# Setup loads, modulation products, gates and relu squared in an adaLN transformer block: what moves when they change place

## What is computed

```python
mod = silu(c) @ wmod                   # c (2, 512), wmod (512, 6*512): sa, ca, ga, sb, cb, gb
ga, gb = sign * max(abs, 0.25)         # of each gate
h = layernorm(x) * (1 + ca) + sa
q, k, v = silu(h @ wq), sigmoid(h @ wk), h @ wv      # 4 heads of 128
f = 1 - k;  theta = pi * cumsum(sign(f - 0.5))       # rotation by 0 or pi: a sign
S = S * f + k v^T;  o = q S            # gated scan over 4096 steps
o = layernorm(o * sigmoid(h @ wg1 @ wg2)) * norm_w
x = x + ga * (o @ wo)
h = layernorm(x) * (1 + cb) + sb
hp = h shifted by one step in time
r = sigmoid((mu_r * h + (1 - mu_r) * hp) @ W_r.T)
k = (mu_k * h + (1 - mu_k) * hp) @ W_k.T
x = x + gb * r * (square(relu(k)) @ W_v.T)
```

## Time and profile before

| | us |
|---|---|
| median of 3 runs | 1885.78 |
| lowest and highest | 1882.69, 1887.09 |
| the profiled execution, its own time | 1883.84 |
| its span in the profile | 1881.9 |
| TensorE busy in the span | 1836.1 |
| VectorE, ScalarE, GpSimd busy | 1457.9, 696.8, 391.4 |
| granted TensorE clock, mean | 0.994 |

### The profile page before, as it was taken

One profiled execution on the slowest core, in us unless ns is written; L12 is line 12 of the kernel. 1 busy time (PEld: TensorE's weight loads), 2 busy tenths in 40 slices (PEclk: granted clock), 3 DMA queues, 4 the chain that ended last, 5 costly groups with the idle time before them and its releaser, 6 DMA issues. The chain is left out here.

```text
span 1881.9 us, 56458 instructions
## 1 busy us (share of the span) xinstructions
PE 1836.1 (98%) x24873; PEld 1648.7 (88%) x24873; DVE 1457.9 (77%) x2885; ACT 696.8 (37%) x1360; POOL 391.4 (21%) x309
## 2 busy tenths in 40 slices
PE   5899999999999999999999999998999999999999
PEld 5789998999989998899988999887888888888887
DVE  4577777677777777777777777778899889889886
ACT  2243334333343333333333333343334434433433
POOL 1001100111011100111001110012244444344343
PEclk9899999999999999999999999999999999999999
DMA  7010100001000010001100011002111111111110
GB/s 280 3 47 25 47 25 25 24 28 43 25 25 24 33 39 25 24 25 36 35 25 24 25 37 35 24 26 68 60 53 68 68 51 62 68 57 57 68 57 34
DMA packets 42650, 84.88 MB, mean 45 GB/s; under 512 B 2324, under 2 KB 2856, under 8 KB 42408
## 3 DMA queue, kind: packets, MB, share of 16 engines
q1 hardware_dynamic: 38552, 74.46, 11.3%
q10 hardware_dynamic: 3856, 6.82, 1.0%
HBM read 47.72 MB, written 33.55 MB: 43 GB/s over the span
## 5 line engine op out<-in xcount | busy, mean ns | idle before, releaser
L130 POOL TENSOR_TENSOR ln_rs<-ln_ve,mhalf 128x2 f32<-128x2 f32 x64 | 71.2, 1113 | 1011.1 <-DVE ln_ve L125 1011.1
L324 POOL TENSOR_TENSOR xs<-xs,y 128x512 f32<-128x512 f32 x64 | 83.5, 1305 | 368.3 <-DVE y L697 368.3
L1099 PE MATMUL bank<-hT_hi,wq_hi 128*128 128x256 f32 x512 | 152.5, 298 | 4.4 <-DVE wq_lo L1043 4.4
L1099 PE MATMUL bank<-hT_hi,wk_hi 128*128 128x256 f32 x512 | 151.4, 296 | 0.0
L730 DVE TENSOR_TENSOR Tot<-Tot 128x256 f32<-128x256 f32 (+2 forms) x192 | 47.1, 245 | 129.4 <-PE lvl L1176 99.1
L136 DVE TENSOR_SCALAR xn<-xs,ln_mv,ln_rs 128x512 f32<-128x512 f32 x128 | 123.5, 1006 | 29.5 <-POOL ln_rs L130 29.5
L1099 PE MATMUL bank<-hT_lo,wq_hi 128*128 128x256 f32 x512 | 146.3, 286 | 0.0
L1099 PE MATMUL bank<-hT_hi,wq_lo 128*128 128x256 f32 x512 | 145.9, 285 | 0.0
L1099 PE MATMUL bank<-xk_hi,fk_hi 128*128 128x256 f32 x512 | 145.1, 283 | 0.6 <-DVE xk_lo L829 0.6
L1099 PE MATMUL bank<-xk_hi,fk_lo 128*128 128x256 f32 x512 | 144.9, 283 | 0.0
L1099 PE MATMUL bank<-xk_lo,fk_hi 128*128 128x256 f32 x512 | 144.9, 283 | 0.0
(11 more groups left out here) (179 smaller groups left out, 5630.2 us busy)
## 6 DMA issues: line engine op xcount, KB each, us to landing
xs<-in_L_attn_x SPq DMA_DIRECT2D x32, 512.0 KB, 3.6
x_scratch<-xs SPq DMA_DIRECT2D x32, 512.0 KB, 3.2
xs<-x_scratch SPq DMA_DIRECT2D x32, 512.0 KB, 3.5
out<-xs SPq DMA_DIRECT2D x31, 512.0 KB, 2.8
mod_raw<-in_L_wmod SPq DMA_DIRECT2D x4, 1024.0 KB, 15.6
mod_raw<-in_L_wmod ACTq DMA_DIRECT2D x2, 1024.0 KB, 14.2
raw_q<-in_L_attn_wq ACTq DMA_DIRECT2D x1, 1024.0 KB, 12.5
raw_k<-in_L_attn_wk SPq DMA_DIRECT2D x1, 1024.0 KB, 14.3
```

Of the source, the lines that this page charges most:

```text
L130: pool.tensor_tensor(out=ln["rs"][:, :], in0=ln["ve"][:, :], in1=mhalf[:, :], op=ALU.pow).then_inc(ln["rstd"], 1)
L324: pool.tensor_tensor(out=dst, in0=dst, in1=y[:, ch, :], op=ALU.add).then_inc(x2_sb, 1)
L1099: last = pe.matmul(dst, lhs(a, s), rhs(b, s), start=(t == 0), stop=(t == len(terms) - 1))
```

## The change

- **Loads.** SA, wq, wg1, wg2, wo and GB leave ScalarE's queue; SyncE issues all the large ones in the order CA, SA, wq, wk, (wait for the first modulation product) wv, wg1, wg2, x of block 1, wo, GA, GB, CB, SB. ScalarE runs one sigmoid on a constant column (`warm`) ahead of the one that is needed. W_k and W_r are issued at the end of block 2.
- **Prologue.** xn of block 1 is turned and the mean of wo made ahead of the gate rows; ScalarE makes h of block 1 ahead of the gate sigmoids.
- **Modulation products.** GA stays behind the near scores; GB, CB and SB stand after the second q rows, the first k rows and the second k rows of block 0, each ahead of a level product. `second_mods` and gate a's diagonal move behind VectorE's update of level 16, centring wo becomes `centre_wo` in the old place, all of wo's low part is made after g1's.
- **Gates.** Gate a is spread in block 0 in the two places where gate b was. Gate b's diagonal is made at the end of block 0 and spread in blocks 1 and 2, one batch each, after the k rows.
- **relu squared.** The square is a ScalarE activation right behind each relu; VectorE has none.

Context lines are thinned out, and the code is shifted left by eight columns:

```diff
@@ -182,12 +182,13 @@
 csig = at("csig", [P, B * KT], 134.5)
-csil = at("csil", [P, B, KT], 134.625)
+csil = at("csil", [P, B, KT], 1.46875)
 mean_m = at("mean_m", [P, P], 135)
...
 nwm = at("nwm", [P, KT, P], 148)
-diag = [at(f"diag{n}", [P, B * KT, P], kb) for n, kb in enumerate((154, 186))]
+diag = [at(f"diag{n}", [P, B * KT, P], kb) for n, kb in enumerate((178, 202))]
+warm = at("warm", [P, 1], 206.5)
 graw, gmag, gsgn = (at(name, [P, 2 * B * KT], 206 + n / 8) for n, name in enumerate(("graw", "gmag", "gsgn")))
@@ -286,11 +287,17 @@
         mod_load(CA)
+        mod_load(SA)
+        rows_in(w_raw["q"], env["wq"], w_in["q"])
         rows_in(w_raw["k"], env["wk"], w_in["k"])
...
         rows_in(w_raw["v"], env["wv"], w_in["v"])
+        rows_in(w_raw["g1"], env["wg1"], w_in["g1"])
+        rows_in(w_raw["g2"], env["wg2"], w_in["g2"])
         ln_load(sp, ln, xf, 1)
+        rows_in(w_raw["o"], env["wo"], w_in["o"])
         mod_load(GA)
+        mod_load(GB)
         mod_load(CB)
@@ -494,6 +501,11 @@
 
+        def square(m, pair):
+            part = rl[:, 2 * pair:2 * pair + 2, :].rearrange("p k t -> p (k t)")
+            act.wait_ge(relu, 2 * m + pair + 1)
+            act.activation(part, part, ACT.Square).then_inc(sq, 1)
+
         def ka_high(m, pair):
@@ -519,20 +531,19 @@
                 q_gate(n + 1, 1 - par, pair)
-            if n == 0:
-                gate_copy(0, bank[0])
-                gate_copy(1, bank[1])
             k_and_f(n + 1, 1 - par, 0)
+            if n == LAST - 1:
+                weight_high("k")
+            k_and_f(n + 1, 1 - par, 1)
+            if n in (1, 2):
+                gate_copy(n + 1, bank[1])
+            v_copy(n + 1, 1 - par, 0)
+            spread_diagonal(n)
+            merge_32(n, par)
             if n == 0:
...
                 act.copy(W["o"][0][:, :, :], w_raw["o"][:, :, :]).then_inc(w_hi["o"], 1)
-            if n == LAST - 1:
-                weight_high("k")
-            k_and_f(n + 1, 1 - par, 1)
-            v_copy(n + 1, 1 - par, 0)
-            spread_diagonal(n)
-            merge_32(n, par)
             if n == LAST - 1:
@@ -540,7 +551,7 @@
             if n == 0:
-                gate_copy(2, bank[3])
+                gate_copy(0, bank[3])
             for ch in range(chunks_kept(n)):
@@ -548,8 +559,8 @@
             if n == 0:
-                gate_copy(3, bank[1])
-                act.wait_ge(w_lo["o"], KT)
+                gate_copy(1, bank[1])
+            if n == 2:
                 for name in "kr":
@@ -562,8 +573,10 @@
             relu_of(0, 0)
+            square(0, 0)
             spread_diagonal(n)
             relu_of(0, 1)
+            square(0, 1)
             merge_32(n, par)
@@ -577,7 +590,9 @@
             relu_of(1, 0)
+            square(1, 0)
             relu_of(1, 1)
+            square(1, 1)
             ogt_high(n, 1)
@@ -586,6 +601,7 @@
                     relu_of(m, pair)
+                    square(m, pair)
                 for pair in range(2):
@@ -607,10 +623,8 @@
         act.dma_start(vrows[(B + 2) * KT:(B + 3) * KT, :], env["mu_k"].rearrange("(k p) -> k p", p=P)).then_inc(small_in, 16)
-        act.dma_start(mod_raw[SA][:, :, :], wmod[:, SA * E:(SA + 1) * E].rearrange("(k p) n -> p k n", p=P)).then_inc(mod_in[SA], 16)
-        for name in ("q", "g1", "g2", "o"):
-            act.dma_start(w_raw[name][:, :, :], env["w" + name].rearrange("(k p) n -> p k n", p=P)).then_inc(w_in[name], 16)
-        act.dma_start(mod_raw[GB][:, :, :], wmod[:, GB * E:(GB + 1) * E].rearrange("(k p) n -> p k n", p=P)).then_inc(mod_in[GB], 16)
+        act.wait_ge(step_pool, 2)
+        act.activation(warm[:, :], mhalf[:, 0:1], ACT.Sigmoid)
         act.wait_ge(vec_sb, 1)
@@ -629,11 +643,11 @@
         g1_high(0)
+        h_affine(1)
         for ch in range(NC):
...
         act.copy(mean_sb[:, :], lbank[0][:, :]).then_inc(mean_copied, 1)
-        h_affine(1)
         for n in range(LAST):
@@ -691,7 +705,7 @@
             dve.wait_ge(rstdo, n + 1)
-            if n == 0 or fresh(n):
+            if n == 0:
                 dve.wait_ge(gab_set, 2)
@@ -836,11 +850,6 @@
 
-        def square(m, pair):
-            part = rl[:, 2 * pair:2 * pair + 2, :]
-            dve.wait_ge(relu, 2 * m + pair + 1)
-            dve.tensor_tensor(out=part, in0=part, in1=part, op=ALU.mult).then_inc(sq, 1)
-
         def ka_low(m, pair):
@@ -878,6 +887,8 @@
                                      op0=ALU.add, op1=ALU.mult).then_inc(gates_set, 1)
+
+        def centre_wo():
             dve.wait_ge(mean_copied, 1)
@@ -907,10 +918,10 @@
                 if m == 1 and n == 0:
+                    centre_wo()
+                if m == 16 and n == 0:
                     second_mods()
                     spread_ready(0)
-                if m == 4 and n == 0:
-                    spread_ready(1)
                 if 1 < m <= 16:
@@ -926,14 +937,13 @@
                     weight_low("k", [m // 32])
-                if n == 0 and m == 32:
-                    split_low_o([0])
             apply_next(n + 2)
...
             if n == 0:
-                split_low_o([1, 2, 3])
+                split_low_o(range(KT))
+                spread_ready(1)
             if n > 0:
@@ -982,8 +992,6 @@
             ln_var(dve, ln, n + 2)
-            square(0, 0)
-            square(0, 1)
             weight_low("v", [1, 2, 3])
@@ -1004,8 +1012,6 @@
             apply_next(n + 3)
-            square(1, 0)
-            square(1, 1)
             ogt_low(n, 1)
@@ -1015,8 +1021,6 @@
             if m > 1:
-                for pair in range(2):
-                    square(m, pair)
                 for pair in range(2):
@@ -1230,10 +1234,9 @@
                 pe.wait_ge(gate_sb, 2)
-                for i in range(2, 6):
-                    mod_product(i, bank[1])
+                mod_product(2, bank[1])
             if n == 1:
-                pe.wait_ge(gab_set, 4)
+                pe.wait_ge(gab_set, 2)
             if n > 0:
@@ -1247,25 +1250,32 @@
             rows_of("q", 1, 2, "q")
+            if n == 0:
+                mod_product(3, bank[1])
             level_product(n, par, 3)
-            if n == 0:
-                pe.wait_ge(h_full, 8)
-                spread_gates(0, 0, bank[0])
-                spread_gates(0, 1, bank[1])
             if n > 0:
...
             rows_of("k", 0, 4, "k")
+            if n == 0:
+                mod_product(4, bank[1])
             level_product(n, par, 4)
...
             rows_of("k", 1, 4, "k")
+            if n == 0:
+                mod_product(5, bank[1])
+            if n in (1, 2):
+                pe.wait_ge(ogt_lo, 2 * n)
+                spread_gates(1, n - 1, bank[1])
             level_product(n, par, 5)
...
             wait(pe, ogt_lo, 2 * n)
-            if n == 0:
-                pe.wait_ge(gab_set, 2)
             v_rows(0)
             level_product(n, par, 6)
+            if n == 0:
+                pe.wait_ge(diag_set, 1)
+            if n in (1, 2):
+                pe.wait_ge(gab_set, n + 2)
             v_rows(1)
@@ -1277,7 +1287,7 @@
                 pe.wait_ge(q_sb, 2 * (n + 2))
-                spread_gates(1, 0, bank[3])
+                spread_gates(0, 0, bank[3])
             pe.wait_ge(level, NU * (n + 1))
@@ -1296,7 +1306,7 @@
             else:
-                pe.wait_ge(gab_set, 3)
+                pe.wait_ge(gab_set, 1)
             for ch in range(chunks_kept(n)):
@@ -1307,7 +1317,7 @@
                 pe.wait_ge(gate_sb, 2 * (n + 2))
-                spread_gates(1, 1, bank[1])
+                spread_gates(0, 1, bank[1])
             pe.wait_ge(s_mid, n + 1)
@@ -1429,20 +1439,21 @@
         g1_rows()
-        pe.wait_ge(g1_lo, 1)
-        pe.wait_ge(w_lo["g2"], 1)
-        pe.wait_ge(v_sb, 2)
-        for ch in range(NC):
-            gate_rows(ch)
+        pe.wait_ge(k_f, 2)
+        pe.wait_ge(v_sb, 1)
+        t1(1)
         pe.wait_ge(mod_set, 2)
...
         last.then_inc(mean_ready, 1)
-        pe.wait_ge(k_f, 2)
-        pe.wait_ge(gate_sb, 1)
-        t1(1)
+        pe.wait_ge(g1_lo, 1)
+        pe.wait_ge(w_lo["g2"], 1)
+        pe.wait_ge(v_sb, 2)
+        pe.wait_ge(h_full, 8)
+        for ch in range(NC):
+            gate_rows(ch)
         for n in range(LAST):
```

## The result

| | before | after |
|---|---|---|
| median in the comparison | 1885.30 us (4 runs) | 1873.28 us (4 runs, 1871.95 to 1875.95) |
| ratio to before | 1 | 0.9939, 95% interval 0.9922 to 0.9956 |
| the profiled execution | 1883.84 us | 1875.95 us |
| its span | 1881.9 us | 1874.0 us |

The change gained 12.0 us at the medians; forecast were 1870.9 us and a gain of 14.9. So a ledger made from them adds up to 7.9, and most of the edits were also run one by one.

What follows compares the result with a forecast made beforehand. TensorE, busy in 98% of the span, was taken as the bound. Terms -6.0 - 0.9 - 4.1 + 0 + 1.2 + 0 + 0.1 - 5.2 = -14.9 us took the median from 1885.8 to 1870.9 us, range 1865 to 1879.

Steps and rivals of the forecast that it cites:

- Part 1: Start: loads on one queue and warm-up activation start the first product near 7.3 us, the stop keeping its length; -6.0 us.
- B: Rival at the start: the stop shortens, second product ends near 12.3 us, 3 us better, 1867.9 us; chance 0.15.
- C: Rival at the start: the stop lasts while the DMA engines are full, only 1 us gained, 1875.9 us; chance 0.12.
- Part 2: Prologue: transposes and the mean of wo ahead of the gate rows cover the wait for g1's low part; -0.9 us.
- Part 3: Block 0: spreading the four modulation products lets instruction packets arrive in time, 9.7 us for 13.8; -4.1 us.
- Rival A: Products stay instruction-bound wherever they stand (0 for -4.1) and the clock falls once more (+2.1): 1877.1 us; chance 0.20.
- one slow stretch: Block 0's clock: one stretch at half clock as before, 0 us, between -1.7 and +4.2.
- Part 4: Blocks 0 to 2: moved gate spreads net 0; VectorE late for diagonal, level of 64 and g1's low part, +1.2 us.
- Part 5: Squares on ScalarE: crossing stalls shrink to 1.9 and 1.7 us (-2.4), no clock falls (-2.8); together -5.2 us.
- rival D: Crossing: the clock falls all the same and only the 2.4 us come, 1873.7 us; chance 0.08.
- the signs that I had named for being right: They included, for the crossing, both stalls below 2 us with the clock at 1.0.
- E: Rival in the feed-forward blocks: Square needs another activation table, +39 us in all, 1910 us; chance 0.03.

Runs made afterwards that it cites:

- experiment 8: Only the prologue's new order (transposes and mean ahead of the gate rows), on the kernel before: 1886.35 us, ratio 0.9991.
- Experiment 3: The changed kernel with the four later modulation products in a row again behind the near scores: 1877.30 us, ratio 0.9946.
- experiment 4: The changed kernel with modulation products 128 columns per matmul, a quarter of the instructions: 1887.98 us, ratio 1.0005.
- experiment 6: The changed kernel with modulation products 64 columns per matmul, half the instructions: 1871.18 us, ratio 0.9908.
- experiment 5: The changed kernel with the W_k and W_r loads issued earlier in block 2, ahead of its v copies: 1874.14 us, ratio 0.9921.
- kernels 7 and 8: 7: only the squares on ScalarE, on the kernel before: 1884.98 us, ratio 0.9985. 8 is experiment 8.
- experiments 1, 2, 8 and 4: 2: the changed kernel with the squares back on VectorE: 1878.92 us, ratio 0.9953. The others are experiment 1, experiment 8 and experiment 4.
- experiment 1: The kernel before with only the loads on one queue and the warm-up sigmoid: 1881.87 us, ratio 0.9970.

## Why the prediction was right, and where it was not

**Part 1, the start (-6.0 forecast, -5.3 in the ledger, -5.2 by itself).** Right in its mechanism: the next wait was for data, then the stop that keeps its length (7.67 us after the product's start, 7.43 before; 7.12 to 7.76 in all nine profiles that have it). That refutes B, in which it shortens, and C, in which it lasts until the DMA engines are free. By its own numbers, 7.3 for 13.58, the term was -6.3 and not -6.0. The term's fault: the first product started at 8.05, not 7.3. The sum of the rates was right (1.62 MB had moved at 7.2 us here too), but 1.95 MB had moved when the product started: I took the bytes moved for the landing of this matrix, while part of them belonged to the loads issued behind it, by my reading.

**Part 2 (-0.9, measured -1.3; -1.55 by itself).** Right in direction, and larger than the one wait it was read from; the interval of experiment 8 just reaches no change. The same stretch differs by up to 0.8 us between profiles of kernels with the same code there, which is as much as the excess. The g_lo entry of 0.9 that the view of waits still has belongs to the gate rows of the next block, in block 0.

**Part 3 (-4.1).** Right, and the strongest step. Its stated 9.7 us holds 4.5 us of idleness, where two pieces of 2.1 are 4.2; the trace has 4.3, and the products with it take 9.5 us, for 14.0 before: the first product kept its stop (2.09), the second lost it, the third handed it to the level product behind it (2.21), the fourth lost it. Experiment 3 puts the four back in a row and gets 7.6 us of idleness and 3.8 us more in block 0. Experiments 4 and 6 remove instructions, leave every byte of data where it is, and the stops of these products vanish. That speaks against the rule of the Trainium skill, "Runtime: NRT & Kernel Launch", Instruction fetch mechanics, that the crossing of a 16 KiB block is "mostly hidden": here each costs 1.6 to 2.7 us when what lies between two crossings runs for 1.25 us. Rival A falls with it. The clock fell in two places in block 0, 53 to 59 (0.72) and 70.8 to 75.4 us (0.63), where one slow stretch had been taken, each behind a stop of 2 us: this is the +2.1 for one more slow stretch, inside my bounds, and the reason why block 0 gave 3.8 of 4.9.

**Part 4 (gates 0, VectorE +1.2).** The gates' two spreads came back as 0.97 and 0.96 us in blocks 1 and 2: net 0. VectorE was late by 0.42 us for the diagonal and 0.22 for the level of 64, and the wait for g1's low part grew from 0.7 to 0.9: together 0.9 of the +1.2, each near what was said (0.5, 0.4, 0.3). What failed here is a sentence of this part: W_k and W_r "move to block 2, a thousand microseconds before use". I priced the loads by their use, not by what else was on the DMA queues. They drain into block 3 and delay the instructions of a level product: 0.64 us of idleness, block 3 +0.9 (experiment 5).

**Part 5, the crossing (-5.2 forecast; -2.8 measured by itself, -2.1 in the ledger).** This is the step that failed. Half of it was right: the Kt stall went from 3.1 to 0.8 (forecast 1.9), and the clock stayed at 1.00 behind it. The other half was wrong. I let the ogT stall shrink to 1.7 because two squares leave the place ahead of its low part, and beside that counted the 1.4 us that the clock gives back behind the Kt stall. But TensorE meets the ogT stall behind that stretch. What it gained there it waits for again: its way from the end of the Kt stall to the ogT stall went from 20.29 to 18.89 us, VectorE's from 23.20 to 21.26, and the stall only from 2.9 to 2.4. The stretch from TensorE's arrival at Kt to the end of the ogT stall still gave 4.2 us, for the 3.8 that these terms come to. What is missing is the clock. Behind the ogT stall it fell (0.72, as before), where I had expected it to stay up. And it fell once more, at 1277, in this profile and not in the one before. So half of rival D came true, and of the signs that I had named for being right, this is the one that did not show. Checked against the ledger: -5.2, +1.4 for the slow stretch that stayed, +0.7 for the ogT stall, -1.1 for the Kt stall, +2.3 for the one at 1277 (the wo products took 5.33 us for 3.00), -0.6 for a wait for xk's low part that is then covered, makes -2.5, and -2.1 is what stands there. The feed-forward half cost nothing but 0.3 us at its end, and E did not happen: Square (0.63 us for 128 x 512) runs on the table that was loaded.

**What stays open.** The fall behind the 2.2 us stall at the start of the crossing, at 1277 in the changed kernel, shows in ten of the twelve profiles, kernels 7 and 8 among them, which have the loads and the products as before; the first wo rows there take 4.5 to 5.4 us. Only the kernel before and experiment 4 kept the clock (3.00 and 2.98 us), and both profiles are of executions faster than their kernel's median. The ogT stall shows the same: the clock fell behind it in eight profiles (stalls of 2.4 to 2.9 us) and stayed up in four, experiments 1, 2, 8 and 4 (2.25 to 2.42 us). So nothing shows the fall at 1277 to be a cost of the change, my reading of the earlier trace rows, that a stall of 2.2 us is safe, was drawn from an exception, and what decides it I can't say: the code of the stretch at 1277 is the same in all twelve. The steady blocks take 39.17 us in all profiles but those of the kernel before and of experiment 1, which have 39.11: kernels 7 and 8 don't touch these blocks either, so the +1.4 us of the ledger can't be put down to one edit. Where it comes from stays open.

**The sum.** The forecast median, 1870.9, is 2.4 us from the measured 1873.28, with the missing 3 us of the crossing and 0.9 of block 3 against it. In its favour worked that issue idleness of the row of products was 7.2 us in the one profile I read, and 7.6 to 9.2 in four other kernels that have it in a row: with the products spread it is 4.3 to 5.1 in four profiles, so spreading saves about 3.4 us in the mean, for the 2.9 of the two profiles compared. The single edits come to 5.2, 2.8 and 1.7 us by themselves, and the products to 1.3 (ratios) or 3.8 (block 0): 11.0 to 13.5, beside 12 to 14 for the whole. That the total came out so near is in part luck: the crossing fell short by half, and the two profiled executions, which the parts are read from, differ by only 7.9 us.

## What to carry to other kernels

A row of short matmuls is priced by instructions as much as by columns: where "issue" idleness stands between them, count instructions per microsecond, put dense work between, or widen the tile. Here 64 columns were the best of three widths, and at 128 the products cost more than the stops had. Loads that nobody waits for can still delay someone, because instructions come over the same DMA engines (the instruction queue stands among them in the earlier trace rows): here it helped to place them in a stretch of long matmuls. And a stall is the difference of two ways, that of the engine that waits and that of the work it waits for. When an edit shortens both, the stall keeps its length though the edit pays: measure both ways from one common landmark, and don't add a gain on the waiting engine to one on the other.

## What the runs showed of the hardware that was not expected

- The same fp32 product, 512 x 512 by 2 columns of data, takes 1.25 us with weight tiles of 32 columns (128 matmuls in the trace), 2.03 with 64 (64) and 3.73 with 128 (32): 10, 32 and 117 ns for one matmul, all in block 0. The four narrow ones that stand for a wide one take together a third of its time.
- At the start a matmul takes twice its later time: 13.78 us for 64 wide ones, 215 ns each, for 117 in block 0. The view prints a granted clock of 1.00 there, but only because the trace has no clock record before 27.5 us (33.1 in the kernel before, 24.2 in experiment 6). The q rows of the changed kernel show the step, at the very time of that first record: equal matmuls start 0.21 us apart before it and 0.12 after.

```profile
26.96 0.41 PE L1103 MATMUL bank<-hT_lo,wq_hi 128*128 128x256 f32 x1
27.17 0.41 PE L1103 MATMUL bank<-hT_hi,wq_lo 128*128 128x256 f32 x1
...
27.70 0.28 PE L1103 MATMUL bank<-hT_hi,wq_lo 128*128 128x256 f32 x1
27.82 0.28 PE L1103 MATMUL bank<-hT_hi,wq_hi 128*128 128x256 f32 x1
```

  What runs before that step runs at half speed. A narrow modulation product took 1.88 us at the start, as it did in the earlier trace rows where the clock is recorded at half, for 1.25 at the full clock.
- One table load serves Sigmoid, Identity, Relu and Square.
- An instruction stop of the narrow products lasts 1.6 to 2.7 us with idle DMA engines and 3.1 to 4.6 at the start with them full. Counted from the first product's start the latter ends after 7.43 us before and 7.67 after the change, though these starts lie 5.5 us apart.
- The stall of TensorE of 2.2 us at the start of the crossing was followed by half clock in ten of twelve profiled executions, 1.5 to 2.4 us each time, the ogT stall of 2.25 to 2.9 us in eight of twelve. The Kt stall was followed by it in all four with 3.1 us and in none of the eight with 0.8 to 0.9.
